# Cross-attention on one core: VectorE adds tile 7's probabilities into tile 6's before TensorE sums them

## The chip, the cores and the metric

The kernel runs on one core of a Trainium2 chip. The metric is the device time of one execution in microseconds (us), the median over the runs shown. Times of single instructions, and the stretches quoted below, come from one profiled execution.

## What is computed

Layer norm of x (2 batches of 512 tokens, 1024 channels, float32), a query projection, attention with 32 heads of 32 channels over 1024 context tokens (keys and values are both the context), an output projection and the residual:

```
x = (hidden_states - mu) * jax.lax.rsqrt(var + LN_EPS) * ln_gamma + ln_beta
Q = _split_heads(x @ Wq.T)
scores = jnp.einsum('bhsd,bhtd->bhst', Q, K) * scale
scores = jnp.where(mask, scores, -jnp.inf)
probs = jax.nn.softmax(scores, axis=-1)
attn = jnp.einsum('bhst,bhtd->bhsd', probs, V)
out = attn @ Wout.T
return residual + out
```

The change concerns the denominator of the softmax: for every head and query, the sum of the exponentials over the 1024 context tokens.

## The kernel before

The attention runs in 16 steps (`STEPS`); a step is one batch and a group of four heads. In a step the 1024 context tokens are eight tiles of 128 (tt = 0 to 7), and a slot of the step handles one tile. For a tile and a head TensorE makes scores of 128 tokens by 512 queries (`score`, L968), ScalarE makes their exponentials in the buffer PR (`exp`, L636, four of 128x512 to a tile), and TensorE multiplies them with the values into PV (`values`, L984). PR holds four tiles (`RING`), so that tile tt lies in place tt % 4; tile 6 lies in place 2 and tile 7 in place 3, and tiles 2 and 3 of the next step write over them.

The scores need a maximum for each query and head, which is found one step ahead. TensorE makes 128x1024 scores of the next step in one of the two PSUM buffers MX (`max_item`, L946), and VectorE takes the maximum of each row (`maximum`, L758), 16 items to a step. The items of a step stand in the table `STEP`; each is written in the MX buffer that the item but one before it used, so that TensorE waits for VectorE to be done with that one (`mx_freed`). Besides the maxima there are in each step "keys" (a transposition of the keys of the step but one ahead: ScalarE's copy L562, VectorE's `key_low` L721, and behind it `split_queries`, L751 and L753, from which SyncE copies rows into R for the maxima of slot 6), "bias" and "sums". In slot 0 stand maxima 4 and 5 and the keys, in slot 1 "sums" and maximum 6:

```
STEP = [
    (maxima(1, 4), maxima(1, 5), keys(2)),
    ([], sums(-1), maxima(1, 6)),
    (maxima(1, 7), [], maxima(1, 8)),
```

The sum over the tokens has two parts. GpSimd adds tiles 0 to 5 into `acc` by five instructions of 128x2048 (`add_probs`, L507), each waiting for the one before it and for the tile's exponentials. When they are done, and the sums of the step before have been inverted, it scales the attention of the step before (`normalise`, L495). TensorE then sums over the 128 partitions with a matrix of ones (`row_sums` and `sum_probs`, L974): tile 6, tile 7 and `acc`, each by four matmuls, one a head, into the free half of an MX buffer. It does so for step n in slot 1 of step n + 1. VectorE turns the result (`invert_sums`, L774, L777, L780).

All queues are in an order written out by hand. On TensorE, slot 0 is: scores 0 and 1, maximum 4, values of the old tile 7, maximum 5, scores 2 and 3, keys. Slot 1 is: scores 0 and 1, values of tile 0, the row sums of the step before, scores 2 and 3, maximum 6. On VectorE it is maximum 4, maximum 5, `key_low`, `split_queries`, the turned sums, maximum 6. GpSimd's first add of a step waits for the exponentials of tile 1, so for scores 2 and 3 of slot 1.

Steps 1 to 12 run in a hardware loop of four steps, steps 13 to 15 are written out. In step 15 there are no maxima; VectorE splits the output weights (L805, L807). Behind it comes the output projection (`project_out`, L1102), whose left operand VectorE splits by `split_attn` (L844, L846); the row sums of step 15 stand behind the first two halves of it.

Of the kernel before, what the change touches and what calls it, by code (L numbers as in the profile page):

```python
# [26 lines left out]
ALU = mybir.AluOpType  # L27
# [8 lines left out]
STEPS = GROUPS * BATCH  # L36
# [5 lines left out]
RING = 4  # L42
# [9 lines left out]
PROBS = TT * HPG  # L52
# [13 lines left out]
DIRECT_TILES = (6, 7)  # L66
# [20 lines left out]
def wout(o):  # L87
    return [("wout", 0, o)]
# [10 lines left out]
def sums(a):  # L99
    return [("sums", a, 0)]  # L100
# [28 lines left out]
def is_first(n):  # L129

    return isinstance(n, int) and n == 0


def items_of(n):

    items = [tuple([i for i in part if n + i[1] < STEPS] for part in slot) for slot in (FIRST_STEP if n == 0 else STEP)]
    if n == STEPS - 2:
        items[TT - 1] = ([], wout(0), wout(1))
    if n == STEPS - 1:
        items = [([], [], []) for _ in range(TT)]  # L140
        for o, tt in zip(range(2, WOUT_BLOCKS), (1, 2, 3, 5, 6, 7)):
            items[tt] = ([], sums(-1) if tt == 1 else [], wout(o))
    return items


def flat(items):
    return [i for slot in items for part in slot for i in part]
# [41 lines left out]
def build(nc, x, ctx, mask, wq, wout, gamma, beta, out):  # L189
    def sb(name, shape, dt):  # L190
        return nc.alloc_sbuf_tensor(name, shape, dt)
# [35 lines left out]
    PR = sb("PR", [P, RING, HPG, S], F32)  # L227
    XS = PR[:, :, :, :].rearrange("p a b c -> p (a b c)").rearrange("p (t c) -> p t c", t=TOK_TILES)
    acc = sb("acc", [P, HPG, S], F32)
# [34 lines left out]
    sem = nc.alloc_semaphore  # L264
# [16 lines left out]
    sums_turned, recip_ready = sem("sums_turned"), sem("recip_ready")  # L281
    scores_ready, exp_done, tile_used, pool_used = sem("scores_ready"), sem("exp_done"), sem("tile_used"), sem("pool_used")
    gate = sem("gate")
    pv_done, pv_copied, sums_done, rsum_done, attn_done = (
        sem("pv_done"), sem("pv_copied"), sem("sums_done"), sem("rsum_done"), sem("attn_done"))
    wo_in = [sem(f"wo_in{g}") for g in range(2)]
    wo_ready, wo_hi = sem("wo_ready"), sem("wo_hi")
    xr_in = [sem(f"xr_in{q}") for q in range(2)]
# [17 lines left out]
    with nc.Block() as block:  # L306
# [372 lines left out]
        def _(dve):  # L679
# [39 lines left out]
            def key_low(n, par):  # L719
                dve.wait_ge(kt_hi, n + 1)  # L720
                nc.vector.tensor_tensor(KTl[:, :], MX[par][:, :], KTh[:, :].bitcast(F32), ALU.subtract).then_inc(kt_lo, 1)  # L721
                dve.wait_ge(kt_lo, n + 1)
                dve.sem_inc(mx_freed, 1)
# [23 lines left out]
            def split_queries(n):  # L747
                if not is_first(n):
                    dve.wait_ge(queries_in, STACKED * n)
                q = QA[:, bass.ds(n, 1), :].rearrange("p a s -> p (a s)")  # L750
                nc.vector.tensor_copy(QTh, q).then_inc(qt_hi, 1)  # L751
                dve.wait_ge(qt_hi, n + 1)
                nc.vector.tensor_tensor(QTl, q, QTh.bitcast(F32), ALU.subtract).then_inc(qt_lo, 1)  # L753

            def maximum(n, u, i, par):

                dve.wait_ge(m_ready, M_ITEMS * n + i + 1)
                nc.vector.tensor_reduce(mx[:, u % 2, i:i + 1], MX[par][:, :], mybir.AxisListType.X, ALU.max,  # L758
                                        negate=True).then_inc(mx_freed, 1)

            def bias_low(n, par):

                dve.wait_ge(bt_hi, n + 1)
                nc.vector.tensor_tensor(BTl[:, :], MX[par][0:M_ITEMS, 0:P], BTh[:, :].bitcast(F32), ALU.subtract).then_inc(bt_lo, 1)
                dve.wait_ge(bt_lo, n + 1)
                dve.sem_inc(mx_freed, 1)

            def invert_sums(n, part, bank=None):


                if part == 0:
                    dve.wait_ge(sums_done, n + 1)
                    dve.wait_ge(attn_done, 1 + n)
                    nc.vector.transpose(rsum[:, :], bank).then_inc(sums_turned, 1)  # L774
                if part == 1:
                    dve.wait_ge(sums_turned, n + 1)
                    nc.vector.reciprocal(rcol[:, :], rsum[:, :].rearrange("p (b i) -> p b i", i=DVE_T)[:, :, 0]).then_inc(recip_ready, 1)  # L777
                if part == 2:
                    dve.wait_ge(recip_ready, n + 1)
                    nc.vector.transpose(rsum[:, :].rearrange("p (b i) -> p b i", i=DVE_T),  # L780
                                        rcol[:, :].unsqueeze(2).to_broadcast([P, S // DVE_T, DVE_T])).then_inc(rsum_done, 1)
# [19 lines left out]
            def wout_parts(o, par):  # L801
                half, n = divmod(o * P, S)
                src = MX[par][:, :].rearrange("p (g n) -> p g n", n=P)
                dve.wait_ge(wo_ready, o + 1)
                nc.vector.tensor_copy(WOh[half][:, :, n:n + P], src).then_inc(wo_hi, 1)  # L805
                dve.wait_ge(wo_hi, o + 1)
                nc.vector.tensor_tensor(WOl[half][:, :, n:n + P], src, WOh[half][:, :, n:n + P].bitcast(F32),  # L807
                                        ALU.subtract).then_inc(mx_freed, 1)

            def step(n, u, items, at, first=False):  # L810
                for tt, slot in enumerate(items):
                    for kind, a, i in flat([slot]):
                        if kind == "keys":
                            key_low(n + a, at % 2)
                            if not first:
                                split_queries(n + a)
                        if kind == "bias":
                            bias_low(n + a, at % 2)
                        if kind == "wout":
                            wout_parts(i, at % 2)  # L820
                        if kind == "max":
                            maximum(n + a, u + a, i, at % 2)
                        if kind == "sums":
                            invert_sums(n + a, 0, MX[at % 2][:, 0:S])
                            dve.wait_ge(sums_turned, n + a + 1)
                            dve.sem_inc(mx_freed, 1)
                        at += 1
                    if tt in SUMS_AT and not first:
                        invert_sums(n - 1, 1 + SUMS_AT.index(tt))

            split_queries(2)
            step(0, 0, FIRST_STEP, FIRST_PARITY, first=True)
            with dve.Fori(0, LOOPS) as j:
                for u in range(1, RING + 1):
                    n = RING * j + u
                    step(n, u, STEP, step_parity(u))
            for n in APART[:-1]:
                step(n, n % RING, items_of(n), step_parity(n))
            n = STEPS - 1
            step(n, n % RING, items_of(n), LAST_PARITY)  # L840

            def split_attn(t, q):
                src = QAt[:, :, bass.ds(t * P, P)]
                nc.vector.tensor_copy(AH[q][:, :, :], src).then_inc(ah_done, 1)  # L844
                dve.wait_ge(ah_done, t + 1)
                nc.vector.tensor_tensor(AL[q][:, :, :], src, AH[q][:, :, :].bitcast(F32), ALU.subtract).then_inc(al_done, 1)  # L846
# [13 lines left out]
            for part in range(3):  # L860
                invert_sums(STEPS - 1, part, SX[0][:, :])
# [12 lines left out]
        def _(pe):  # L874
# [96 lines left out]
            def sum_probs(bank, tile, start, stop):  # L971

                for h in range(HPG):
                    ins = nc.tensor.matmul(bank[h * HD:(h + 1) * HD, :], ones[:, :], tile(h), start=start, stop=stop,  # L974
                                           skip_group_check=True)
                return ins

            def values(n, u, tt):

                pe.wait_ge(exp_done, PROBS * n + HPG * (tt + 1))  # L980
                if tt == 0 and not is_first(n):
                    pe.wait_ge(pv_copied, n)
                for h in range(HPG):
                    ins = nc.tensor.matmul(PV[h * HD:(h + 1) * HD, :], C[u % RING][:, tt, h * HD:(h + 1) * HD],  # L984
                                           PR[:, tt % RING, h, :], start=(tt == 0), stop=(tt == TT - 1), skip_group_check=True)
                if tt == TT - 1:
                    ins.then_inc(pv_done, 1)
                if tt in POOL_TILES:
                    ins.then_inc(tile_used, 1)

            def row_sums(n, bank):

                for tt in DIRECT_TILES:
                    sum_probs(bank, lambda h: PR[:, tt % RING, h, :], tt == DIRECT_TILES[0], False).then_inc(tile_used, 1)
                pe.wait_ge(pool_used, ADDS * n + 2 * ADDS)
                sum_probs(bank, lambda h: acc[:, h, :], False, True).then_inc(sums_done, 1)

            def before_step_0(at):

# [87 lines left out]
            with pe.Fori(0, LOOPS) as j:  # L1087
                for u in range(1, RING + 1):
                    n = RING * j + u
# [3 lines left out]
            n = STEPS - 1  # L1093
# [49 lines left out]
```

## Time and profile before

| | |
|---|---|
| median of 3 runs | 700.71 us (698.27 to 701.65) |
| profiled execution, its own time | 698.58 us |
| profiled execution, first to last instruction | 696.8 us |
| TensorE matmul busy | 664.4 us (95%) |
| VectorE busy | 454.1 us (65%) |
| GpSimd busy | 392.6 us (56%) |
| ScalarE busy | 339.1 us (49%) |
| TensorE row sums (L974) | 376 matmul records, 47.0 us of busy time (28.5 + 15.6 + 1.9 + 1.0) |
| granted TensorE clock | 1.000 over the span, the 2.4 GHz level |

Each float32 matmul of L974 and L984 stands in the trace as two records, so that the four matmuls of a tile are eight. The attention steps take the stretch from about 150 to 603 us; the layer norm and the projection of the queries stand ahead of them, the output projection behind.

### The profile page before, as it was taken

The numbers are of one execution on the slowest core, as the hardware profiler recorded it, in microseconds if no ns is written. First come the engines' busy times: TensorE is split into PE (matmuls) and PEld (weight loads), VectorE is DVE, ScalarE is ACT, GpSimd is POOL, SyncE is SP. The second block draws the span as 40 slices with busy tenths as digits, with TensorE's granted clock in tenths as the row PEclk, the third lists the DMA queues.
The fourth block names the chain that finished last, engine by engine and source line by source line (L and its number), as shares of the span: only waits on it lengthen the run. The fifth ranks groups of instructions, "written<-read, shape, count | busy, mean of one in ns | idle before, by whom it ended". The sixth has DMA issues, their size and how long they took to land.

```text
span 696.8 us, 10761 instructions
## 1 busy us (share of the span) xinstructions
PE 664.4 (95%) x3537; PEld 390.2 (56%) x3537; DVE 454.1 (65%) x494; ACT 339.1 (49%) x614; POOL 392.6 (56%) x107
## 2 busy tenths in 40 slices
PE   2799999989999999999999999999999999899998
PEld 2577787844444454454544445444544454578886
DVE  6764343059878788787887878878878676733231
ACT  3741121255566666566666657566675666400000
POOL 1000000057588797887977979779797798900000
PEclk9999999999999999999999999999999999999999
DMA  9712000344615426154261442624515104033131
GB/s 343 203 36 72 31 31 1 74 121 119 151 48 137 101 69 160 42 133 106 62 166 47 121 116 60 158 57 111 131 37 136 62 11 143 31 120 121 60 120 60
DMA packets 40286, 68.10 MB, mean 98 GB/s; under 512 B 5668, under 2 KB 22694, under 8 KB 40238
## 3 DMA queue, kind: packets, MB, share of 16 engines
q1 hardware_dynamic: 39956, 67.25, 35.2%
q10 hardware_dynamic: 292, 0.40, 0.2%
q8 instruction: 17, 0.28, 0.2%
q14 instruction: 21, 0.17, 0.1%
HBM read 25.18 MB, written 4.19 MB: 42 GB/s over the span
## 4 chain that ended last, share of the span: by engine, by line
PE 88%; DVE 4%; ACT 3%; SPq 2%; DMA 1%; issue 1%; POOL 0%; ACTq 0%; DVEq 0%; POOLq 0%
PE MX L946 19%; PE SX L968 18%; PE PV L984 18%; PE MX L1102 13%; PE MX L974 6%; PE SX L909 5%; PE PV L909 5%; PE MX L886 2%; PE SX L901 1%; PE MX L956 1%; DMA PR<-in_x 1%; ACT PR L546 1%; PE MX L880 1%; ACT PR L636 1%; DVE R L717 1%
## 5 line engine op out<-in xcount | busy, mean ns | idle before, releaser
L758 DVE TENSOR_REDUCE mx<-MX 128x1 f32<-128x1024 f32 x256 | 302.6, 1215 | 75.9 <-PE MX L946 69.8
L636 ACT ACTIVATE PR<-SX 128x512 f32<-128x512 f32 x512 | 268.9, 601 | 146.2 <-PE SX L968 140.2
L507 POOL TENSOR_TENSOR acc<-acc,PR 128x2048 f32<-128x2048 f32 x64 | 294.1, 4596 | 8.7 <-POOL acc L507 7.6
L507 POOL TENSOR_TENSOR acc<-PR 128x2048 f32<-128x2048 f32 x16 | 73.4, 4590 | 208.9 <-ACT PR L636 208.9
L968 PE MATMUL SX<-R 99*128 99x512 f32 x512 | 173.5, 418 | 3.2 <-ACT PR L636 3.0
L946 PE MATMUL MX<-R 97*128 97x512 f32 x512 | 170.6, 416 | 4.7 <-DMA R<-R 1.6
L968 PEld LDWEIGHTS SX<-R 99*128 99x128 f32 x512 | 89.8, 188 | 89.3 <-ACT PR L636 64.3
L984 PE MATMUL PV<-PR,C 128*32 128x512 f32 x1024 | 136.4, 605 | 0.1
L946 PEld LDWEIGHTS MX<-R 97*128 97x128 f32 x512 | 88.7, 190 | 67.4 <-DVE mx L758 47.1
L855 DVE TENSOR_TENSOR PR<-PR,MX 128x512 f32<-128x512 f32 x16 | 10.9, 686 | 53.3 <-PE MX L1102 51.8
L984 PEld LDWEIGHTS PV<-PR,C 128*32 128x32 f32 x1024 | 20.1, 108 | 44.8 <-ACT PR L636 28.6
L1102 PE MATMUL MX<-R 128*128 128x512 f32 x192 | 44.3, 390 | 0.0
L1102 PEld LDWEIGHTS MX<-R 128*128 128x128 f32 x192 | 36.0, 188 | 8.3 <-issue 0.8
L1102 PE MATMUL MX<-R,KTh 128*128 128x512 f32 x128 | 40.2, 390 | 0.0
L909 PE MATMUL PV<-R 128*128 128x512 f32 x120 | 31.3, 408 | 0.2 <-DVE R L717 0.2
L721 DVE TENSOR_TENSOR KTl<-MX,KTh 128x1024 fp32r<-128x1024 f32 x15 | 18.4, 1224 | 18.9 <-ACT KTh L562 18.9
L974 PE MATMUL MX<-PR,ones 128*32 128x512 f32 x240 | 28.5, 592 | 0.0
L1102 PEld LDWEIGHTS MX<-R,KTh 128*128 128x128 f32 x128 | 24.0, 188 | 5.8 <-issue 0.8
L584 ACT ACTIVATE QA<-SX 128x512 f32<-128x512 f32 x8 | 4.8, 598 | 44.3 <-PE SX L909 44.3
L495 POOL TENSOR_TENSOR QA<-QA,rsum 128x512 f32 (+1 forms) x16 | 20.6, 1287 | 9.4 <-issue 9.4
L909 PE MATMUL SX<-R,KTh 128*128 128x512 f32 x80 | 25.5, 389 | 0.0
L1102 PE MATMUL MX<-R,KTl 128*128 128x512 f32 x64 | 24.9, 389 | 0.0
(84 smaller groups left out, 472.6 us busy)
## 6 DMA issues: line engine op xcount, KB each, us to landing
R<-KTh SPq DMA_DIRECT2D x60, 256.0 KB, 4.2
PR<-in_x SPq DMA_DIRECT2D x16, 512.0 KB, 4.1
C<-in_ctx SPq DMA_DIRECT2D x16, 512.0 KB, 3.4
R<-QT SPq DMA_DIRECT2D x62, 128.0 KB, 2.5
R<-KTl SPq DMA_DIRECT2D x60, 128.0 KB, 3.8
acc<-in_L_xattn_Wq SPq DMA_DIRECT2D x8, 512.0 KB, 3.7
C<-in_L_xattn_Wout SPq DMA_DIRECT2D x8, 512.0 KB, 3.4
R<-QT SPq DMA_DIRECT2D x62, 64.0 KB, 2.1
```

The source lines that it names most:

```text
L495: nc.gpsimd.tensor_tensor(at, at, rsum[:, :], ALU.mult).then_inc(attn_done, 1)
L507: nc.gpsimd.tensor_tensor(acc[:, :, :], a, PR[:, tt % RING, :, :], ALU.add).then_inc(pool_used, 1)
L636: nc.scalar.activation(PR[:, tt % RING, h, :], SX[bank(HPG * tt + h)][:, :], ACT.Exp, scale=SCALE).then_inc(exp_done, 1)
L721: nc.vector.tensor_tensor(KTl[:, :], MX[par][:, :], KTh[:, :].bitcast(F32), ALU.subtract).then_inc(kt_lo, 1)
L758: nc.vector.tensor_reduce(mx[:, u % 2, i:i + 1], MX[par][:, :], mybir.AxisListType.X, ALU.max, negate=True).then_inc(mx_freed, 1)
L886: ins = nc.tensor.transpose(MX[par][:, t * P:(t + 1) * P], C[u % RING][:, t, :], ident[:, :])
L909: ins = nc.tensor.matmul(QP[b if bank is None else bank][:, :], w[W_IN[g]][:, k * P:(k + 1) * P], v[b][:, k, :], start=(k == 0 and o == 0) ...
L946: ins = nc.tensor.matmul(MX[par][:, cs], QS[u % RING][0:BIAS, h, st * P:(st + 1) * P], KS[u % RING][0:BIAS, h, cs], start=True, stop=True)
L968: nc.tensor.matmul(SX[bank(at)][:, :], KS[u % RING][0:ROWS, h, tt * P:(tt + 1) * P], QS[u % RING][0:ROWS, h, :], start=True, stop=True).th ...
L974: ins = nc.tensor.matmul(bank[h * HD:(h + 1) * HD, :], ones[:, :], tile(h), start=start, stop=stop, skip_group_check=True)
L984: ins = nc.tensor.matmul(PV[h * HD:(h + 1) * HD, :], C[u % RING][:, tt, h * HD:(h + 1) * HD], PR[:, tt % RING, h, :], start=(tt == 0), sto ...
L1102: ins = nc.tensor.matmul(MX[1 - q][:, cs], a[q][:, g, :], w[half][:, g, :], start=(g == 0 and o == 0), stop=(g == GROUPS - 1 and o == 2))
```

## The change

A new function `add_pair` on VectorE adds tile 7's probabilities to tile 6's, in place in PR, in two halves of two heads (128x1024 elements each, both inputs in SBUF). Each half waits until all exponentials of the step are there and until TensorE has read tile 6 for the values (`pair_read`). The halves stand behind maximum 4 and behind maximum 5 in slot 0 of the next step, in step 15 both ahead of its first item, and for step 15 itself behind all its items, ahead of `split_attn`. TensorE's `row_sums` now sums `acc` first, then waits for both halves (`pair_added`) and sums the pair: eight matmuls in place of twelve. Both places of PR are given free together behind that.

```diff
+            def add_pair(n, half):
+
+                hs = slice(2 * half, 2 * half + 2)
+                a, b = (PR[:, tt % RING, hs, :] for tt in DIRECT_TILES)
+                dve.wait_ge(exp_done, PROBS * n + PROBS)
+                dve.wait_ge(pair_read, n + 1)
+                nc.vector.tensor_tensor(a, a, b, ALU.add).then_inc(pair_added, 1)
...
             def step(n, u, items, at, first=False):
                 for tt, slot in enumerate(items):
+                    if tt == 0 and isinstance(n, int) and n == STEPS - 1:
+                        for half in range(2):
+                            add_pair(n - 1, half)
...
                             maximum(n + a, u + a, i, at % 2)
+                            if tt == 0 and not first:
+                                add_pair(n - 1, i - 4)
...
             step(n, n % RING, items_of(n), LAST_PARITY)
+            for half in range(2):
+                add_pair(n, half)
...
                 if tt in POOL_TILES:
                     ins.then_inc(tile_used, 1)
+                if tt == DIRECT_TILES[0]:
+                    ins.then_inc(pair_read, 1)
 
             def row_sums(n, bank):
 
-                for tt in DIRECT_TILES:
-                    sum_probs(bank, lambda h: PR[:, tt % RING, h, :], tt == DIRECT_TILES[0], False).then_inc(tile_used, 1)
                 pe.wait_ge(pool_used, ADDS * n + 2 * ADDS)
-                sum_probs(bank, lambda h: acc[:, h, :], False, True).then_inc(sums_done, 1)
+                sum_probs(bank, lambda h: acc[:, h, :], True, False)
+                pe.wait_ge(pair_added, 2 * n + 2)
+                sum_probs(bank, lambda h: PR[:, DIRECT_TILES[0] % RING, h, :], False, True).then_inc(sums_done, 1)
+                pe.sem_inc(tile_used, 2)
```

VectorE at the start of a step of the loop, with the semaphores each instruction waits for (L758 the maxima, L721 `key_low`, L751 and L753 `split_queries`, L774 the turned sums). Before:

```order
L758 TENSOR_REDUCE mx<-MX 128x1 [waits m_ready]
L757 REGISTER_ALU
L758 TENSOR_REDUCE mx<-MX 128x1 [waits m_ready]
L720 REGISTER_ALU
L721 TENSOR_TENSOR KTl<-MX,KTh 128x1024 [waits kt_hi]
L749 ISA [waits kt_lo]
L751 ISA [waits queries_in]
L751 COPY QT<-QA 128x512
L753 TENSOR_TENSOR QT<-QA,QT 128x512 [waits qt_hi]
```

With the change (here L774 is `add_pair`):

```order
L758 TENSOR_REDUCE mx<-MX 128x1 [waits m_ready]
L772 ISA
L773 REGISTER_ALU [waits exp_done]
L774 TENSOR_TENSOR PR<-PR 128x1024 [waits pair_read]
L757 REGISTER_ALU
L758 TENSOR_REDUCE mx<-MX 128x1 [waits m_ready]
L774 TENSOR_TENSOR PR<-PR 128x1024 [waits pair_read,exp_done]
L720 REGISTER_ALU
L721 TENSOR_TENSOR KTl<-MX,KTh 128x1024 [waits kt_hi]
```

The two halves stand ahead of maximum 5 and of `key_low`, and so ahead of all that follows these.

TensorE in slot 1 of a step of the loop, from the row sums to scores 2. Before:

```order
L974 MATMUL MX<-PR,ones 32x512 [waits mx_freed]
L974 MATMUL MX<-PR,ones 32x512 x7
L995 ISA
L974 MATMUL MX<-acc,ones 32x512 [waits pool_used]
L974 MATMUL MX<-acc,ones 32x512 x3
L965 REGISTER_ALU
L968 MATMUL SX<-R 128x512 [waits exp_done]
```

With the change (L989 is the body of `sum_probs`):

```order
L989 MATMUL MX<-acc,ones 32x512 [waits pool_used]
L989 MATMUL MX<-acc,ones 32x512 x3
...
L989 MATMUL MX<-PR,ones 32x512 [waits pair_added]
L989 MATMUL MX<-PR,ones 32x512 x3
```

Four matmuls of eight on PR are gone, and those on PR are now last and wait for VectorE. The orders of ScalarE and GpSimd are the same as before.

## Rows read from the trace of the kernel before

**Rows 1.** The page's head and its busy times
```profile
span 696.8 us, 10761 instructions
PE 664.4 (95%) x3537; PEld 390.2 (56%) x3537; DVE 454.1 (65%) x494; ACT 339.1 (49%) x614; POOL 392.6 (56%) x107
```

**Rows 2.** The chain that ended last, shares by engine
```profile
PE 88%; DVE 4%; ACT 3%; SPq 2%; DMA 1%; issue 1%; POOL 0%; ACTq 0%; DVEq 0%; POOLq 0%
```

**Rows 3.** Busy us of each engine in one step, then clock and DMA
```profile
211.00:239.60 28.60, 28.60 (x163) 13.87 (x162) 22.86 (x24) 18.48 (x36) 24.19 (x6) 1.00 0.42 103
```

**Rows 4.** Timeline around row sums: start us, us, engine, line, op; [idle before <-releaser]
```profile
319.29 1.23 DVE L758 TENSOR_REDUCE mx<-MX 128x1 f32<-128x1024 f32 x1 [0.21 <-PE MX L946]
321.46 0.13 PEld L974 LDWEIGHTS MX<-PR,ones 128*32 128x32 f32 x4 [0.30 <-issue]
...
323.17 0.13 PEld L974 LDWEIGHTS MX<-acc,ones 128*32 128x32 f32 x4 [0.30 <-issue]
...
324.57 0.30 PEld L968 LDWEIGHTS SX<-R 99*128 99x128 f32 x2 [0.84 <-issue]
...
326.27 4.59 POOL L507 TENSOR_TENSOR acc<-PR 128x2048 f32<-128x2048 f32 x1 [3.78 <-ACT PR L636]
```

**Rows 5.** Timeline of POOL alone, steps 1, 5, 14 and 15
```profile
182.43 4.59 POOL L507 TENSOR_TENSOR acc<-PR 128x2048 f32<-128x2048 f32 x1 [11.54 <-ACT PR L636]
...
297.66 4.59 POOL L507 TENSOR_TENSOR acc<-PR 128x2048 f32<-128x2048 f32 x1 [4.61 <-ACT PR L636]
...
316.66 4.58 POOL L507 TENSOR_TENSOR acc<-acc,PR 128x2048 f32<-128x2048 f32 x1 [0.16 <-POOL acc L507]
321.20 1.29 POOL L495 TENSOR_TENSOR QA<-QA,rsum 128x512 f32 x1
...
555.24 4.58 POOL L507 TENSOR_TENSOR acc<-PR 128x2048 f32<-128x2048 f32 x1 [3.69 <-ACT PR L636]
559.91 18.56 POOL L507 TENSOR_TENSOR acc<-acc,PR 128x2048 f32<-128x2048 f32 x4
...
582.73 4.58 POOL L507 TENSOR_TENSOR acc<-PR 128x2048 f32<-128x2048 f32 x1 [3.02 <-ACT PR L636]
```

**Rows 6.** Timeline of DVE alone, start of a step
```profile
315.59 3.49 DVE L758 TENSOR_REDUCE mx<-MX 128x1 f32<-128x1024 f32 x3 [0.42 <-PE MX L946]
...
321.77 1.23 DVE L721 TENSOR_TENSOR KTl<-MX,KTh 128x1024 fp32r<-128x1024 f32 x1 [1.26 <-ACT KTh L562]
...
323.93 0.69 DVE L753 TENSOR_TENSOR QT<-QA,QT 128x512 fp32r<-128x512 f32 x1
```

**Rows 7.** Lines L846 and L753: ns min/median/max, first and last start us
```profile
L846 DVE TENSOR_TENSOR KTl<-QA,KTh x4: 1225/1226/5509, 605.4 to 673.2; 128x1024 fp32r<-128x1024 f32 x4
L846 DVE TENSOR_TENSOR R<-QA,R x3: 1224/1225/1226, 622.4 to 662.3; 128x1024 fp32r<-128x1024 f32 x3
...
L753 DVE TENSOR_TENSOR QT<-QA,QT x16: 691/693/694, 46.4 to 524.2; 128x512 fp32r<-128x512 f32 x16
```

**Rows 8.** Timeline of all engines at the end of the attention
```profile
599.99 9.80 POOL L507 TENSOR_TENSOR acc<-acc,PR 128x2048 f32<-128x2048 f32 x2
...
604.65 0.68 DVE L844 CAST KTh<-QA 128x1024 fp32r<-128x1024 f32 x1
605.37 5.51 DVE L846 TENSOR_TENSOR KTl<-QA,KTh 128x1024 fp32r<-128x1024 f32 x1
614.42 0.16 PEld L974 LDWEIGHTS SX<-PR,ones 128*32 128x32 f32 x8 [0.35 <-issue]
```

**Rows 9.** SyncE's last query rows, their landing, and the maximum that needs them
```profile
335.24 0.59 SPq L341 DMA_DIRECT2D R<-QT  x1
...
R<-QT SPq DMA_DIRECT2D x62, 64.0 KB, 2.1
...
311.65 0.72 PE L946 MATMUL MX<-R 97*128 97x512 f32 x2
```

More of the change, by code:

```diff
@@ L283, in build @@
     gate = sem("gate")
-    pv_done, pv_copied, sums_done, rsum_done, attn_done = (
-        sem("pv_done"), sem("pv_copied"), sem("sums_done"), sem("rsum_done"), sem("attn_done"))
+    pv_done, pv_copied, sums_done, rsum_done, attn_done, pair_read, pair_added = (
+        sem("pv_done"), sem("pv_copied"), sem("sums_done"), sem("rsum_done"), sem("attn_done"), sem("pair_read"), sem("pair_added"))
     wo_in = [sem(f"wo_in{g}") for g in range(2)]
```

## Prediction

> **What bounds the kernel now.** I read the page's busy times first, then the chain of waits, then one step in the timeline, engine by engine. TensorE is busy for 664.4 of 696.8 us [rows 1], it makes 88% of the chain that ended last [rows 2], and in a step of 28.60 us it is busy throughout, beside 22.86 us of VectorE and 24.19 of GpSimd [rows 3]. So an edit that takes matmuls away should shorten each step, as long as neither of the other two comes to end a wait later. GpSimd is nearer to that than its 56% of the span tells. Call S the start of its first add in a step and E the end of its fifth. S is 297.66 and, a step later, 326.27: a period of 28.61 us. E is 316.66 + 4.58 = 321.24, so the adds take E - S = 23.58 us [rows 4, 5]. From E to the next S only 5.03 us are left, and GpSimd sits idle for 3.78 us of them, waiting for exponentials whose scores TensorE issues behind the row sums [rows 4]. Whatever makes that piece longer makes the period longer, however much slack there is elsewhere.
>
> **TensorE's part.** The weight loads of tile 6 start at 321.46 and those of acc, two tiles later, at 323.17 [rows 4]: 1.71 us for two tiles, 0.86 us each. One tile of three goes, in 16 steps: 16 x 0.86 = 13.8 us, all of it on the path as long as TensorE bounds the steps.
>
> **VectorE's part: the plain cost.** An add of 128x1024 float32 with both inputs in SBUF is in the trace, at L846: 1.225 us [rows 7]. Two of them are 2.45 us a step, 39 us in all; 22.86 + 2.45 = 25.3 us still fits in a period of 27.7. If this were all, it would lie beside TensorE's work: maximum 4 is the last of the three that end at 315.59 + 3.49 = 319.08 [rows 6], the halves and maximum 5 would be done at 322.8, and TensorE, which could start the pair at 321.46 + 0.86 = 322.3, would wait some 0.5 us at most, part of it paid by starting later anyway.
>
> **VectorE's part: the wait at GpSimd.** One row says that the add costs more. Six of the seven L846 take 1.225 us, the first took 5.509 [rows 7]. It started at 605.37 and ended at 610.88. GpSimd's last add ended at 599.99 + 9.80 = 609.79, and 1.09 us later the VectorE instruction was done, about its whole own length [rows 8]. So it did not share with the GpSimd add; it stood until that had ended. The 16 instructions of L753, also with two SBUF inputs, never took more than 0.694 us [rows 7], but the one at 323.93 runs where GpSimd is idle, between 321.20 + 1.29 = 322.49 and 326.27 [rows 4 to 6]. The maxima, which read PSUM, run beside GpSimd's adds at 3.49 us for three [rows 6]. The first half of `add_pair` is of the kind that stood. It comes up behind maximum 4, at 319.08, while GpSimd's fifth add runs from 316.66 to 321.24. So it will stand until E.
>
> The Trainium skill states the rule ("SBUF — State Buffer", Who interferes with whom): a VectorE instruction with two SBUF inputs contends with a GpSimd instruction that reads SBUF, and the later one is blocked for the whole of the other. The row of 5.51 us agrees. By this rule the sum is the one worked out below; without it, it would be that of rival 2.
>
> **The new loop.** From E, in order:
> - the first half ends at E + 1.09 [rows 8];
> - maximum 5 takes 1.23 more [rows 4]: E + 2.32. Meanwhile `normalise` (1.29 us [rows 5], two SBUF inputs as well) runs from E + 1.09 to E + 2.38;
> - the second half, 1.23: E + 3.55. (`normalise` is over 0.06 us after it comes up, which is within this.)
> - a semaphore's way to TensorE, 0 to 0.16 us (GpSimd's gap between two adds that wait for each other is 0.16 [rows 5]): 0.1;
> - from the weight loads of the last summed tile to the next S: 326.27 - 323.17 = 3.10 us [rows 4]. The order behind them is unchanged. The sums of acc are done by then: maximum 5 gives their MX buffer free at E + 2.32, and 0.86 later is E + 3.2.
>
> Sum: 6.75 us in place of 5.03. The period becomes 23.58 + 6.75 = 30.33 us, 1.72 more than 28.61, and TensorE's saved 0.86 us is already in it (without it the wait would not be shorter, since acc stands ahead of the pair).
>
> Is anything else later still? `key_low` ends 1.25 us behind the second half in place of 323.00. From it to the start of L753 it is 2.16 us [rows 6]. So L753 starts 2.2 us behind the second half and ends at 2.9; the next S is 3.2 behind it. It slips in ahead of GpSimd by 0.3 us or, at its start, 1.0. SyncE's row copies for the maxima of slot 6 start with `key_low`, which moves from S - 3.27 to S - 1.95, 1.3 us later against S. The last of them is issued by 335.83 and lands about 2.1 us later, 337.9; the maximum that needs them is at 311.65 + 28.61 = 340.26 [rows 9]. 2.3 us of slack less 1.3 remain. VectorE then lags TensorE by about 1 us in slots 1 to 3, where it waits on TensorE now; maximum 4 comes at most as far behind S as 21.4 + 1, and E is at S + 23.58. So the GpSimd loop closes last, and the first half is always late enough to be caught and never pushes E. ScalarE's order is the same; it gets tiles 2 and 3 of PR free later, but their scores stand behind the row sums anyway.
>
> **Sum over the kernel.**
> - Step 0 to 1: GpSimd is idle for 11.54 us before S of step 1 [rows 5], so no add is caught; the pair is ready in time and S comes 0.86 us earlier.
> - From S of step 1 (182.43) to S of step 14 (555.24) there are 13 periods, 372.81 us. Now 13 x 30.33 = 394.3, less 0.35 in step 13, which is outside the loop and whose adds follow each other faster (559.91 + 18.56 - 555.24 = 23.23 in place of 23.58 shows it for step 14 [rows 5]): +21.1.
> - Step 14 to 15: 582.73 - 555.24 = 27.49 before. Both halves follow each other there; GpSimd's waiting `normalise` can come between them, as the GpSimd add at 604.7 came between L844 and L846 [rows 8]. 23.23 + 1.09 + 1.29 + 1.09 + 0.1 + 3.10 = 29.9, or 28.8 without it. I take the first, +2.4.
> - The end: the halves of step 15 stand until GpSimd is done at about 609.8, L844 and L846 follow to about 614; the row sums are due only at 614.42, behind two halves of the projection [rows 8]. So -0.86.
>
> Together -0.9 + 21.1 + 2.4 - 0.9 = **+21.8 us**. Against the profiled execution's own 698.58 us that is 720.4. The median of the runs shown is 2.1 us above that execution, so against it 722.5. I forecast 722.
>
> **Rivals.**
> 1. **`normalise` goes first at E.** GpSimd's next instruction is dispatched at 321.20, before the adds are even over at 321.24 [rows 5]. If it keeps the way, the first half starts 1.29 us later, and 14 boundaries x 1.29 = +18 us: 740. For it speaks that zero gap; against it that the half has been waiting for 2 us by then. 17%. The same section of the Trainium skill ("SBUF — State Buffer") says that whoever issues first gets the shared pair of ports, which would be the half; no row here shows it at such a meeting.
> 2. **No blocking, the change is a gain.** The first L846 was slow from something else, or only float32r outputs stand. Then TensorE keeps 16 x 0.86 = 13.8 us less up to 0.5 a step for the wait at the pair: 687 to 695. The turning point is whether the first half ends before about E + 0.3. For it speaks only that this is one row of 5.5 us; against it that its end fits GpSimd's to its own length. 11%.
> 3. **L753 is caught as well.** It comes up 1.0 us ahead of S. If it comes behind S, it stands for 4.6 us, and with it the turned sums, an MX buffer and TensorE. Less the 1 us or so of slack that is +3.6 in 13 periods, 47 us: 770. Against it: both hang on the same second half, so that their distance is fixed. 5%.
> 4. **Half and half.** The loop is shorter than reckoned, because TensorE had prepared more behind the wait: 700 to 712. 5%, a third of that within 0.5%.
>
> The forecast's own case has 62%; with 0 to 0.16 for the semaphore, 28.8 or 29.9 in the last step and 0.2 either way in 3.55 it spans 716 to 727. The range takes in rival 1 and the upper part of rival 4: 707 to 741, which leaves out rivals 2 and 3. Within 0.5% (3.5 us, about what a measurement of this kernel can tell) lies 2%; faster 11%; slower 87%.
>
> **What would show it.** In the profile after: `add_pair` with a mean between 1.2 and 3 us in its two places, the first half of 3 to 4.5 us ending 1.1 us behind GpSimd's fifth add; S to S of 30.3 us; GpSimd idle for 5.4 us before S in place of 3.78; TensorE's row sums with two tiles and a wait for VectorE between or ahead of them; its busy share lower. Both halves at 1.23 us would refute the blocking and with it the sign. L753 at 5 us would be rival 3. A first half that ends 2.4 us behind E is rival 1.

## The result and the profile after

The change makes the kernel slower: 714.55 us (median of 4 runs, 714.02 to 714.84) against 700.02 us (4 runs), a ratio of 1.0195 with a 95% interval of 1.0164 to 1.0225. The forecast was 722, with a range of 707 to 741.

The page of the changed kernel, its head, busy times and the chain's shares:

```profile
span 713.0 us, 10609 instructions
PE 662.7 (93%) x3409; PEld 384.4 (54%) x3409; DVE 503.6 (71%) x526; ACT 339.4 (48%) x614; POOL 405.8 (57%) x107
...
PE 66%; DVE 18%; issue 9%; SPq 3%; DMA 2%; ACT 1%; DVEq 1%; POOL 0%; POOLq 0%; ACTq 0%
```

The profiled execution took 714.84 us itself. Its span is 16.2 us longer than before [rows 1], while TensorE is busy for less. VectorE has 49.5 us more to show, of which two adds a step at 1.21 us each explain only 39. In the chain TensorE fell from 88% [rows 2] to 66%, VectorE rose from 4% to 18%.

The costliest groups of the same page (busy us, mean ns of one) have the two that grew:

```profile
L774 DVE TENSOR_TENSOR PR<-PR 128x1024 f32<-128x1024 f32 x32 | 59.3, 1858 | 0.0
...
L495 POOL TENSOR_TENSOR QA<-QA,rsum 128x512 f32 (+1 forms) x16 | 34.3, 2143 | 10.6 <-DVE rsum L788 10.6
```

`add_pair` (L774) has a mean of 1.86 us where one alone takes 1.21, and GpSimd's `normalise` (L495), which the change does not touch, went from 1.29 to 2.14. The timeline of all engines, around the start of one step, says why:

```profile
320.99 4.59 POOL L507 TENSOR_TENSOR acc<-acc,PR 128x2048 f32<-128x2048 f32 x1 [0.16 <-POOL acc L507]
...
324.23 2.43 DVE L774 TENSOR_TENSOR PR<-PR 128x1024 f32<-128x1024 f32 x1
...
325.53 2.26 POOL L495 TENSOR_TENSOR QA<-QA,rsum 128x512 f32 x1
...
326.58 1.21 DVE L758 TENSOR_REDUCE mx<-MX 128x1 f32<-128x1024 f32 x1
...
327.72 1.21 DVE L774 TENSOR_TENSOR PR<-PR 128x1024 f32<-128x1024 f32 x1
...
328.98 0.16 PEld L989 LDWEIGHTS MX<-PR,ones 128*32 128x32 f32 x8 [0.90 <-DVE PR L774]
...
331.68 4.59 POOL L507 TENSOR_TENSOR acc<-PR 128x2048 f32<-128x2048 f32 x1 [3.89 <-ACT PR L636]
```

GpSimd's fifth add ends at E = 320.99 + 4.59 = 325.58. The first half comes up at 324.23 and ends at 326.66, 1.08 us behind E: of its 2.43 us it stood for 1.2. `normalise` comes up at 325.53, behind the half, and ends at 327.79, 2.21 us behind E: it stood in turn until the half was done. The second half finds its way free (1.21 us) and ends at 328.93, E + 3.35; TensorE's weights for the pair follow 0.05 us later; S is 331.68, E + 6.10. The adds themselves are as they were (302.00 to 325.58: 23.58 us). The step before had its S at 302.00, so the period is 29.68 us, as against 28.61 [rows 4, 5].

TensorE now waits where it did not before. Waits of the changed kernel, in total us, times, longest:

```profile
PEld MX L989 <- DVE PR L774: 16.4, 15, 3.0
...
PEld MX L961 <- DVEq L839: 11.9, 13, 1.0
...
PE MX L961 <- DVEq L839: 7.8, 13, 0.6
```

The first is the wait for the pair. The other two are maximum 7 in the MX buffer that VectorE gives back when it has turned the row sums (L839 is that signal): VectorE is late with all that stands behind the second half. In this kernel they do not set the period: GpSimd's adds, from S to E, take the same 23.58 us as before, and from E to S the path is the one just followed. They matter in experiments 1 and 9.

From profile to profile the 16.2 us divide so: S of step 1 is 183.28 for 182.43 (+0.85), the 13 periods to S of step 14 take 568.94 - 183.28 = 385.66 for 372.81 us (+12.9), step 14 to 15 takes 29.35 for 27.49 (+1.9), and the rest 0.6 more.

### The profile page after: what moved, and what is told of

Read it like the earlier page. It is cut to its first block, busy times and chain, and to the rows that moved or that the text cites. A ratio compares the mean times of both kernels' runs of the same rounds, so it can differ in the third digit from the quotient of the medians.

```text
span 713.0 us, 10609 instructions
## 1 busy us (share of the span) xinstructions
PE 662.7 (93%) x3409; PEld 384.4 (54%) x3409; DVE 503.6 (71%) x526; ACT 339.4 (48%) x614; POOL 405.8 (57%) x107
## 4 chain that ended last, share of the span: by engine, by line
PE 66%; DVE 18%; issue 9%; SPq 3%; DMA 2%; ACT 1%; DVEq 1%; POOL 0%; POOLq 0%; ACTq 0%
PE MX L961 15%; PE PV L999 13%; PE MX L1120 12%; PE SX L983 12%; DVE mx L758 6%; PE SX L924 5%; PE PV L924 5%; DVE PR L774 3%; DVE KTl L721 2%; DVE rsum L782 1%; DMA PR<-in_x 1%; DVE QT L751 1%; PE MX L971 1%; PE MX L895 1%; PE SX L916 1%
## 5 line engine op out<-in xcount | busy, mean ns | idle before, releaser
L758 DVE TENSOR_REDUCE mx<-MX 128x1 f32<-128x1024 f32 x256 | 302.4, 1214 | 68.5 <-PE MX L961 60.0
L961 PE MATMUL MX<-R 97*128 97x512 f32 x512 | 172.5, 420 | 12.6 <-DVEq L839 7.8
L774 DVE TENSOR_TENSOR PR<-PR 128x1024 f32<-128x1024 f32 x32 | 59.3, 1858 | 0.0
L495 POOL TENSOR_TENSOR QA<-QA,rsum 128x512 f32 (+1 forms) x16 | 34.3, 2143 | 10.6 <-DVE rsum L788 10.6
L924 PEld LDWEIGHTS PV<-R 128*128 128x128 f32 x120 | 22.4, 196 | 4.7 <-DVE R L717 0.7
```

Source lines behind the costliest of these rows:

```text
L495: nc.gpsimd.tensor_tensor(at, at, rsum[:, :], ALU.mult).then_inc(attn_done, 1)
L774: nc.vector.tensor_tensor(a, a, b, ALU.add).then_inc(pair_added, 1)
L924: ins = nc.tensor.matmul(QP[b if bank is None else bank][:, :], w[W_IN[g]][:, k * P:(k + 1) * P], v[b][:, k, :], start=(k == 0 and o == 0) ...
L961: ins = nc.tensor.matmul(MX[par][:, cs], QS[u % RING][0:BIAS, h, st * P:(st + 1) * P], KS[u % RING][0:BIAS, h, cs], start=True, stop=True)
```

## The experiments

All times stand beside runs of the kernel before on the same chips, whose median was 701.1 for experiments 1 to 4 and 700.9 for the others. "Period" is S to S, the mean over the 13 intervals between steps 1 and 14 in the profiled execution; it is 28.68 us before and 29.67 with the change. Experiments 1, 4, 7 and 9 leave a tile out of the row sums (tile 7, in experiment 4 tile 5), so that their result is not the attention's; they tell only of time.

### 1. The same load with one SBUF input

```diff
-                nc.vector.tensor_tensor(a, a, b, ALU.add).then_inc(pair_added, 1)
+                nc.vector.tensor_reduce(red[:, half:half + 1], b.rearrange("p h s -> p (h s)"), mybir.AxisListType.X, ALU.max,
+                                        negate=True).then_inc(pair_added, 1)
```

> The pair add is replaced, at the same two places and with the same waits, by a maximum over one SBUF input of 128x1024 (tile 7's half), so that tile 7 is left out of the row sums; VectorE's plain load is the same (an instruction of about 1.21 us). Blocking theory (a VectorE instruction with two SBUF inputs stands until GpSimd's add has ended): these take 1.2 us each though GpSimd's fifth add is running, the rows' period falls from 29.67 to about 27.5 us (28.60 less the 1.06 us that one tile of row sums takes), and the time is 700 - 16 x 1.06 = 683, between 682 and 690. Rival, VectorE's load and the new wait themselves are the cost: as the changed kernel, 713 to 716.

Measured: 696.37 us, ratio 0.9943 (0.9925 to 0.9962), period 28.42. Its groups, and VectorE's timeline while GpSimd's fifth add ran (229.86 to 234.45):

```profile
L775 DVE TENSOR_REDUCE red<-PR 128x1 f32<-128x1024 f32 x32 | 38.6, 1210 | 0.0
```

```profile
232.79 1.21 DVE L775 TENSOR_REDUCE red<-PR 128x1 f32<-128x1024 f32 x1
233.92 1.21 DVE L759 TENSOR_REDUCE mx<-MX 128x1 f32<-128x1024 f32 x1
```

Nothing stands when one SBUF input is read, though GpSimd is adding. With the same number of instructions of the same length at the same places the change would have been a small gain. So the blocking costs 18 us (714.55 less 696.37), more than the whole loss. But the time expected was 683, and it is 13 above that: of the saving forecast for the tile only 4 to 5 us came.

### 2. and 3. The add behind maximum 5, in two halves and in one piece

```diff
-                            if tt == 0 and not first:
-                                add_pair(n - 1, i - 4)
+                            if tt == 0 and not first and i == 5:
+                                for half in range(2):
+                                    add_pair(n - 1, half)
```

> Both halves stand behind maximum 5 in place of one ahead of it. Theory (loop from the end of GpSimd's fifth add, E, to its next first add, S): maximum 5 is off the path, but GpSimd's waiting normalise goes between the two halves, as it did from step 14 to 15 of the changed kernel; the second half ends at E + 1.08 + 1.15 + 1.08 = E + 3.3 as against 3.35 now, so the period stays at 29.6 and the time at 713 to 715. Rival: the halves follow each other without normalise between them, E + 2.2, a period of 28.5 and 698 to 700.

For one piece `add_pair` takes all four heads (`PR[:, tt % RING, :, :]`) and TensorE waits for `n + 1`.

> One add of 128x2048 behind maximum 5 in place of two halves. Blocking theory: it stands until E, ends at E + 2.2 (1.2 us for 1024 elements, twice the slope), nothing of GpSimd can go between, and S follows at E + 4.95 in place of 6.10: a period of 28.5 us, so 14 x 1.15 = 16 us less than the changed kernel, 698.5 (697 to 701), no slower than the kernel before. Rival, the load of VectorE and its late maxima set the time: 710 to 715 as now, since the load is nearly the same.

Measured: 715.94 us (ratio 1.0213, 1.0182 to 1.0244), period 29.77, and 713.27 us (1.0178, 1.0153 to 1.0203), period 29.71. For the halves the time is as expected, but not by the way expected; for one piece the expected 698.5 failed. Timelines of GpSimd and of VectorE in the run with one piece:

```profile
318.61 4.58 POOL L507 TENSOR_TENSOR acc<-acc,PR 128x2048 f32<-128x2048 f32 x1 [0.16 <-POOL acc L507]
323.16 1.27 POOL L495 TENSOR_TENSOR QA<-QA,rsum 128x512 f32 x1
```

```profile
322.19 1.23 DVE L758 TENSOR_REDUCE mx<-MX 128x1 f32<-128x1024 f32 x1 [0.21 <-PE MX L958]
323.33 3.25 DVE L773 TENSOR_TENSOR PR<-PR 128x2048 f32<-128x2048 f32 x1
```

GpSimd's fifth add ends at E = 323.19. Maximum 5 keeps VectorE until 323.42, so that the add comes up 0.2 us behind `normalise`. That runs its plain 1.27 us to 324.43, and the add ends 2.15 us later, at 326.58. In the run with two halves it is the same: `normalise` is ahead of both, not between them as was expected. Who comes up first goes first, in both directions: the half that had waited since 324.23 was ahead of `normalise` in the changed kernel, the add that came 0.2 us late is behind it here.

### 4. GpSimd done early

```diff
-POOL_TILES = (0, 1, 2, 3, 4, 5)
+POOL_TILES = (0, 1, 2, 3, 4)
...
-                if tt in POOL_TILES:
+                if tt not in DIRECT_TILES:
```

> GpSimd adds only tiles 0 to 4 (four adds a step), so tile 5 is left out of the row sums; the pair add is as in the change. Blocking theory: GpSimd is done 4.75 us earlier, 2.4 us ahead of the first half, so that nothing stands: both halves take 1.2 us, the period falls to about 27.5 us and the time to 683 to 690. Rival, VectorE's load and wait are the cost: 713 to 716 as now.

Measured: 701.26 us (ratio 1.001, 0.9994 to 1.0026), period 28.43. All 32 halves take 1.21 to 1.22 us. This is the other way to take the collision away, with the real pair add, and the period comes out as in experiment 1. The whole time is 4.9 us above it, though, and neither theory's number. Of the difference between the two profiled executions 4.2 us lie behind S of step 15 and 1.6 between S of step 0 and of step 1, less 1.0 ahead of that. In step 15 GpSimd, with fewer adds, is idle for 4.57 us ahead of `normalise`; that this is the cause there was not tested. The period is this run's result.

### 5. One add, and `normalise` behind it

```diff
                 pool.wait_ge(rsum_done, n + 1)
+                if behind_pair:
+                    pool.wait_ge(pair_added, n + 2)
```

> As the run with one add behind maximum 5, and GpSimd's normalise waits for that add. In that run normalise came up at 323.16, just ahead of the add at 323.33, and the add stood for its 1.29 us: S came 6.2 us behind E. Blocking theory: with normalise behind it the add ends 2.2 us behind its own start (E + 0.2), S follows at E + 5.1, the period falls from 29.72 to 28.6 us and the time by 14 x 1.1 = 15 us, to 698 (696 to 702). Rival, VectorE's plain load holds the period at 29.7: 711 to 714.

Measured, on top of the edit of experiment 3: 700.22 us (ratio 0.9999, 0.9975 to 1.0023), period 28.74. GpSimd, then VectorE:

```profile
317.15 4.58 POOL L509 TENSOR_TENSOR acc<-acc,PR 128x2048 f32<-128x2048 f32 x1 [0.16 <-POOL acc L509]
324.15 1.28 POOL L497 TENSOR_TENSOR QA<-QA,rsum 128x512 f32 x1 [2.43 <-DVE PR L775]
326.62 4.58 POOL L509 TENSOR_TENSOR acc<-PR 128x2048 f32<-128x2048 f32 x1 [1.19 <-ACT PR L638]
```

```profile
321.40 2.48 DVE L775 TENSOR_TENSOR PR<-PR 128x2048 f32<-128x2048 f32 x1
```

The add ends at 323.88, 2.15 us behind E = 321.73, and S follows at E + 4.9. A wait added on GpSimd takes 13 us off experiment 3. The whole loss of the change is gone with the full result computed, but nothing is gained on the kernel before: over the 13 steps S comes 4.9 to 5.6 us behind E, 5.2 in the mean, and with the 23.6 of the adds that is its period again.

### 6. to 8. The tile and the load apart

Three runs keep the order of the change in `row_sums` (acc first, one release for both places of PR). The first has no pair add and sums three tiles:

```diff
                 sum_probs(bank, lambda h: acc[:, h, :], True, False)
-                pe.wait_ge(pair_added, 2 * n + 2)
-                sum_probs(bank, lambda h: PR[:, DIRECT_TILES[0] % RING, h, :], False, True).then_inc(sums_done, 1)
+                sum_probs(bank, lambda h: PR[:, DIRECT_TILES[0] % RING, h, :], False, False)
+                sum_probs(bank, lambda h: PR[:, DIRECT_TILES[1] % RING, h, :], False, True).then_inc(sums_done, 1)
```

The second leaves the last line out, so that tile 7 is in no sum. The third is experiment 1 with three tiles, the wait for `pair_added` ahead of the last.

> No pair add and no wait for one; TensorE sums acc first, then tiles 6 and 7, and gives both places of PR free together: the change's order alone, with the full result. TensorE comes to the sums 0.2 us behind E as it is, so that acc is ready. Both theories: as the kernel before, 699 to 702. More than 704 would mean that the order and the later release cost something of their own.

> As the order alone, but tile 7 is left out of the row sums: eight matmuls for twelve and nothing added to VectorE. Theory L (the saved tile is worth its 0.86 us a step, and VectorE's plain load eats most of it when it is there): 700 - 13.8 = 686 (684 to 688), 10 us below the run with one-input maxima in place of the adds (696.4). Theory M (the tile was never worth that much, since another wait closes when it goes): as that run, 695 to 698.

> The one-input maxima stand where the halves of the pair add stood, so that VectorE has the plain load and nothing stands at GpSimd, and TensorE sums all three tiles: the full result. Theory L (the load by itself costs about 0.7 us a step through the late turned sums and maxima): 700 + 10 = 710 (707 to 713). Theory M (the load is hidden): 699 to 702.

| TensorE sums | VectorE's load | time, us | ratio (95%) | period |
|---|---|---|---|---|
| 3 tiles | none (6) | 701.80 | 1.0019 (0.9992 to 1.0046) | 28.66 |
| 3 tiles | one-input (8) | 701.50 | 1.0005 (0.9981 to 1.0028) | 28.65 |
| 2 tiles | none (7) | 688.46 | 0.9827 (0.9788 to 0.9865) | 27.98 |
| 2 tiles | one-input (1) | 696.37 | 0.9943 (0.9925 to 0.9962) | 28.42 |
| 2 tiles | the change | 714.55 | 1.0195 (1.0164 to 1.0225) | 29.67 |

The last row is the changed kernel. The order costs nothing. The tile is worth 12 us by itself, near the 13.8 reckoned. The load costs nothing as long as TensorE has three tiles to sum, and 8 us once it has two. Experiment 7 came out by theory L (688.5, half a us above its 684 to 688) and experiment 8 by theory M. The load does not add to every period; it puts a floor of 28.4 us under one that would be 28.0 without it and leaves one of 28.65 as it is.

### 9. What the floor is

Experiment 1 again, and VectorE turns the row sums ahead of `split_queries`:

```diff
                             key_low(n + a, at % 2)
-                            if not first:
-                                split_queries(n + a)
+                            split_later = not first
...
                             dve.wait_ge(sums_turned, n + a + 1)
                             dve.sem_inc(mx_freed, 1)
+                            if split_later:
+                                split_queries(n + 2)
```

> As the run with one-input maxima in place of the adds (tile 7 left out), and VectorE turns the row sums ahead of split_queries, not behind it. Theory (the plain load costs time because TensorE waits for the MX buffer that the turned sums give back, 13 waits of 0.3 to 0.4 us in that run and none in the one without the load): that wait goes, the period falls from 28.42 towards the 27.98 us of the run without the load, the time from 696.4 to 690. Rival, VectorE's load holds elsewhere too: 695 to 697. A third way: split_queries, now 0.7 us later, comes up behind GpSimd's first add and stands for 4.6 us: 720 or more, with L753's kind of instruction at 4 to 5 us.

Measured: 689.26 us (ratio 0.9832, 0.9790 to 0.9874), period 28.01. The period of experiment 7 is back, with the load in place. In the waits of experiment 1 stood

```profile
PEld MX L963 <- DVEq L841: 8.5, 13, 0.8
...
PE MX L963 <- DVEq L841: 4.4, 11, 0.4
```

and in this run there is no wait of TensorE for that signal. (Experiment 7, which by the expectation has none, has seven short ones, 1.9 us in all.) So VectorE is not short of time for 2.4 us more in a step; one MX buffer came back late. That is shown for the one-input load.

The third way of the expectation was missed by a hair:

```profile
237.34 0.69 DVE L754 TENSOR_TENSOR QT<-QA,QT 128x512 fp32r<-128x512 f32 x1
237.39 5.08 POOL L508 TENSOR_TENSOR acc<-PR 128x2048 f32<-128x2048 f32 x1 [2.57 <-ACT PR L637]
```

In 12 of the 13 steps the two-input subtraction of `split_queries` starts only 0.03 to 0.05 us ahead of GpSimd's first add, and that add has 5.08 to 5.11 us in place of 4.59. This time it is GpSimd that stands, for half a us, and it has that half to spare.

### 10. The same in the run of experiment 5

> As the run with one add ahead of normalise, and the turned sums ahead of split_queries. The turned sums wait for normalise, which ends 1.6 us behind the add, so that the two-input instruction of split_queries comes up 2.9 us behind the add's end, when GpSimd's next first add has begun at 2.7. Blocking theory (the prediction's rival 3): it stands until that add has ended, at least 4 us in each of 13 steps, and the time rises from 700 to 735 (720 to 755). Rival: it still slips in ahead, or does not stand: 698 to 702.

Measured: 769.65 us (ratio 1.0962, 1.0900 to 1.1024), period 34.07. The line of `split_queries`' subtraction, a two-input instruction that takes 0.69 to 0.70 us in every other run, and one instance of it between its neighbours, on VectorE and on GpSimd:

```profile
L755 DVE TENSOR_TENSOR QT<-QA,QT x16: 691/4898/5026, 46.4 to 590.7; 128x512 fp32r<-128x512 f32 x16
```

```profile
286.71 4.89 DVE L755 TENSOR_TENSOR QT<-QA,QT 128x512 fp32r<-128x512 f32 x1
```

```profile
286.25 4.80 POOL L509 TENSOR_TENSOR acc<-PR 128x2048 f32<-128x2048 f32 x1 [1.18 <-ACT PR L638]
291.21 4.78 POOL L509 TENSOR_TENSOR acc<-acc,PR 128x2048 f32<-128x2048 f32 x1 [0.16 <-POOL acc L509]
```

It came up 0.46 us behind GpSimd's first add, stood until that ended at 291.05, and was done 0.55 us later. This happens in 12 of the 13 steps, in one of them at a start only 0.05 us behind the add's. In the step left over it came up 0.04 us ahead of the add:

```profile
321.15 0.69 DVE L755 TENSOR_TENSOR QT<-QA,QT 128x512 fp32r<-128x512 f32 x1
321.19 5.09 POOL L509 TENSOR_TENSOR acc<-PR 128x2048 f32<-128x2048 f32 x1 [1.72 <-ACT PR L638]
```

From this S to the next it is 28.98 us, where the other 12 periods have 33.8 to 35.1. The same run thus shows both sides of GpSimd's start.

The rise is twice what was expected (69 us for 35), and a row says where more of it comes from. The maxima stand behind the blocked instruction, and TensorE waits for them:

```profile
292.79 1.22 PE L962 MATMUL MX<-R 97*128 97x512 f32 x2 [4.38 <-DVE mx L760]
```

The next exponentials come late, and GpSimd idles for 3.47 us ahead of its third add. Behind TensorE's wait the granted clock was 0.50, the 1.2 GHz level, from 292 to 296 us; over the blocked periods it was about 0.90 in the mean, over the one free period 1.00. What the clock alone costs of the 69 us was not taken apart. A swap of two neighbours on VectorE gains 7 us (experiment 9) or loses 69, by which side of GpSimd's start the two-input instruction falls on.

## Why the prediction was right, and where its sizes were off

The sign and the mechanism hold, step by step: the first half ends 1.08 us behind E (1.09 forecast); `normalise` waits for the half and not the other way, so rival 1 did not come; E - S stays 23.58; L753 slips in ahead of S in all steps (0.691 to 0.694 us; it starts 0.8 us ahead of S, 1.0 forecast), so rival 3 did not come; the loop from E to S is the one that closes last. Experiment 10 shows rival 3 at 770 us, the number the text gave it, but that run is not the change and its rise of 69 us is made up otherwise than the 47 of the text, so that the number agrees by luck. On rule and trace: the Trainium skill's page "SBUF — State Buffer", Who interferes with whom, says that whoever issues first has the shared ports for the whole instruction. The trace of the changed kernel agrees (the half 1.3 us ahead of `normalise`), and so do experiments 3 and 10, where the first came 0.2 and 0.5 us ahead of the other.

The forecast of +21.8 us was too large. The measured +14.5 is from median to median; between the two profiled executions, from which the forecast was added up, it is 16.3, since the one before ran 1.4 us below its median and the one after 0.3 above. Nor did the forecast's own case, 716 to 727, take in the 714.55: it lies in the gap between that and rival 4 (700 to 712, the loop shorter than reckoned), and the range caught it only because it was drawn to take in the upper part of that rival. These terms were off:

- **"from the weight loads of the last summed tile to the next S ... 3.10 us"** measured 2.70 (328.98 to 331.68). In the kernel before, the weights of acc were loaded at 323.17, 0.43 us ahead of the matmuls that use them, while those of tile 7 ran. In the changed kernel, behind the wait, weights and matmuls start together (rows below the list). So the row that I measured from stood early. 0.40 us a period.
- **"the second half, 1.23: E + 3.55"** measured E + 3.35. VectorE's instructions of this size follow each other at 1.13 to 1.14 us, start to start, though each lasts 1.21 (326.58, 327.72, 328.85). 0.20 us a period.
- The semaphore's way was 0.05, not 0.1. The three make 0.65, in 13 periods 8.4 us: forecast +21.1, measured +12.9.
- **The end and the beginning, -0.86 each**: measured +0.6 and +0.85 in the profiled execution. Its granted clock fell in both stretches (last section); where it did not, both terms came as forecast. From S of step 0 to S of step 1 it is 34.74 us before and 33.9 to 34.0 in experiments 1, 2, 3, 5, 7, 9 and 10. From S of step 15 to the end it is 114.07 us before, and 113.20 in experiment 9, the one run with two tiles that has the full clock from there to the end.
- Step 14 to 15 was forecast at +2.4 and came to +1.9, with `normalise` between the halves, as assumed.
- Two of the signs to look for were off as well. The first half was to last 3 to 4.5 us and has 2.4 to 2.6: maximum 4 ends only 1.3 us ahead of E, not 2.2, so that it stands less, which changes nothing at its end. GpSimd was to idle for 5.4 us before S and idles for 3.9, because the time in which `normalise` stands is in its own record (2.26 us in place of 1.29).

For the first term, the matmuls of the last summed tile before, then its weights and matmuls with the change:

```profile
323.60 1.04 PE L974 MATMUL MX<-acc,ones 128*32 128x512 f32 x8
```

```profile
328.98 0.16 PEld L989 LDWEIGHTS MX<-PR,ones 128*32 128x32 f32 x8 [0.90 <-DVE PR L774]
328.98 1.07 PE L989 MATMUL MX<-PR,ones 128*32 128x512 f32 x8
```

The larger error was in a rival. "If this were all, it would lie beside TensorE's work" and the 687 to 695 of rival 2 took VectorE's slack in a period (22.9 + 2.4 in 27.7 us) as enough. Experiment 1 gave 696.4, just above that. I had seen that VectorE "lags TensorE by about 1 us in slots 1 to 3" and let it pass, because GpSimd's loop closed later. Without that loop it is what sets the period, through one MX buffer (experiment 9). Had there been no blocking, the 13.8 us of the tile would have come to a gain of 4 to 5.

## What to carry to other kernels

- An instruction of VectorE with two SBUF inputs is priced by what GpSimd is doing when it comes up, not by its elements: 0.69 us of work took 4.9, nearly the whole of a GpSimd instruction (experiment 10), 1.22 us of work took 5.5 [rows 7]. A distance of 0.04 us ahead of the other's start was enough to be spared. Look for one instance that is out of line with its group in the trace before; here a single row in seven gave the mechanism away.
- When two engines meet like this, the order of arrival decides: with the add in one piece, a wait on the engine that can afford it (experiment 5) took back the whole loss.
- Slack in a period is no cover for a step; what stands behind the new work on its engine, and which buffer it gives back, is.

## What the runs showed that was not expected

The changed kernel runs at a mean granted clock of 0.988 in its profiled execution, the kernel before at 1.000. Stretches of the changed kernel (us, then PE, PEld, DVE, ACT and POOL busy, granted clock, DMA share, GB/s):

```profile
609.00:611.00 2.00, 0.60 (x4) 0.53 (x5) 0.00 (x0) 2.00 (x4) 2.00 (x1) 1.00 0.00 0
611.00:613.00 2.00, 2.00 (x14) 1.35 (x15) 0.90 (x1) 1.21 (x3) 2.00 (x1) 0.59 0.03 8
613.00:615.00 2.00, 2.00 (x9) 0.34 (x6) 1.55 (x2) 0.69 (x2) 2.00 (x2) 0.56 0.75 258
615.00:617.00 2.00, 2.00 (x16) 1.39 (x19) 0.62 (x1) 1.40 (x3) 2.00 (x2) 1.00 0.01 4
```

In step 15 TensorE idles for 1.68 us at one place, in both kernels. In the kernel before it went on at full clock behind it. Here it had also waited 2.13 us for the pair at 595.5, and behind the second idle stretch the clock fell to near the 1.2 GHz level for some 4 us. A values group took 1.94 us there in place of 1.07, about 0.9 us more for one group. A like fall, to 0.50 between 18 and 26 us, stands at the start of this execution and not of the other; nothing of the change runs there. Another, to 0.71 in the mean, lies between 145 and 150 us, where step 0 has its S. The fall in step 15 does not need the adds: experiments 1 and 7, which have none, show 0.50 in their profiled executions at the same place of the step. Nor does every execution have it: experiment 9's has the full clock there. The same kernel differs with the clock by some us: among the runs of the kernel before beside experiments 5 to 8, the four with a mean of 0.985 took 703.0 to 704.2, the two with 0.999 and 1.000 took 698.02. How much of the fall the change causes is open.
